# A graph layer on one core: weights prepared before the first rank on ScalarE, w1l and the first three x + beta on GpSimd

## The reference

```python
h = relu(layernorm(x))
agg = segment_sum(edge_attr, src, num_segments=50000)
g = silu(concat([h, agg], -1) @ W1 + b1)
g = g @ W2 + b2
g = (g - mean(g)) * rsqrt(var(g) + 1e-5) * gamma + beta
out = x + g + h
```

## Time and profile before

| | |
|---|---|
| median of three runs | 710.79 us |
| the profiled execution's own time | 710.52 us |
| its span, first to last instruction | 709.0 us |
| mean granted TensorE clock | 0.984 |
| busy: PE, PEld | 678.2 us (96%), 596.3 us (84%) |
| busy: DVE, ACT, POOL | 685.8 us (97%), 608.4 us (86%), 479.1 us (68%) |

### The profile page before, as it was taken

One profiled execution on the slowest core, in us unless ns is written; L12 is line 12 of the kernel. 1 busy time (PEld: TensorE's weight loads), 2 busy tenths in 40 slices (PEclk: granted clock), 3 DMA queues, 4 the chain that ended last, 5 costly groups with the idle time before them and its releaser, 6 DMA issues.

```text
span 709.0 us, 15612 instructions
## 1 busy us (share of the span) xinstructions
PE 678.2 (96%) x4566; PEld 596.3 (84%) x4566; DVE 685.8 (97%) x2361; ACT 608.4 (86%) x2090; POOL 479.1 (68%) x415
## 2 busy tenths in 40 slices
PE   5999988699999999999999999999999999999993
PEld 2888847599898989898989898999898989889993
DVE  6999879999999999999999999999999999999998
ACT  6999957589898989898989898989898988989883
POOL 5000057687778777777878777778777878777850
PEclk9999989999999999999999999999999999999997
DMA  6000001133333323242424242424232323331212
GB/s 221 1 2 2 1 15 54 52 116 108 112 113 107 118 97 130 87 137 84 140 83 142 83 139 85 141 83 140 85 135 87 129 96 120 106 106 52 81 43 84
DMA packets 28260, 65.90 MB, mean 93 GB/s; under 512 B 8469, under 2 KB 10023, under 8 KB 28174
## 3 DMA queue, kind: packets, MB, share of 16 engines
q1 hardware_dynamic: 15598, 51.90, 20.7%
q0 software_dynamic: 12576, 12.99, 7.5%
HBM read 52.05 MB, written 25.60 MB: 110 GB/s over the span
## 4 chain that ended last, share of the span: by engine, by line
DVE 66%; issue 20%; PE 10%; POOL 1%; DMA 1%; ACT 0%; DVEq 0%; POOLq 0%
DVE T L1138 14%; DVE lo L1126 10%; DVE stat L869 10%; DVE R L1108 8%; DVE R L1133 8%; PE y L671 3%; DVE R L1155 2%; PE za L658 2%; PE pre L665 2%; PE pre L658 2%; PE za L665 1%; DVE guess_off L922 1%; DVE mdd L905 1%; DVE var L908 1%; DVE guess L912 1%
## 5 line engine op out<-in xcount | busy, mean ns | idle before, releaser
L452 POOL DMA_INDIRECT G<-in_edge_attr_dram,slot_edge x388 | 465.2, 1199 | 120.9 <-issue 90.2
L754 PEld LDWEIGHTS y<-w2c,S 128*128 128x128 f32 (+1 forms) x1556 | 188.2, 191 | 8.0
L754 PE MATMUL y<-w2c,S 128*128 128x128 f32 (+1 forms) x1556 | 189.2, 275 | 0.0
L554 ACT ACTIVATE H<-X,shift,rstd 128x128 f32<-128x128 f32 x392 | 161.8, 489 | 4.1 <-DVE shift L927 4.1
L729 PE MATMUL pre<-hi,w1h 128*128 128x512 f32 (+1 forms) x392 | 163.7, 418 | 0.0
L730 PE MATMUL pre<-hi,w1l 128*128 128x512 f32 (+1 forms) x392 | 154.5, 394 | 0.0
L571 ACT ACTIVATE S<-pre,b1c 128x512 f32<-128x512 f32 (+1 forms) x196 | 125.3, 700 | 4.5 <-PE pre L734 4.5
L734 PE MATMUL pre<-lo,w1h 128*128 128x512 f32 (+1 forms) x392 | 122.7, 394 | 0.1
L1126 DVE TENSOR_TENSOR lo<-za,hi 128x1024 fp32r<-128x1024 f32 (+1 forms) x98 | 119.0, 1214 | 2.0 <-ACT hi L564 2.0
L869 DVE BATCH_NORM_STATS2 stat<-X 128x6 f32<-128x128 f32 x392 | 106.7, 280 | 0.1
L715 PE MATMUL za<-HOT,G 128*128 128x128 f32 (+1 forms) x784 | 104.8, 277 | 0.9 <-DMA G<-in_edge_attr_dram,slot_edge 0.9
(11 more groups left out here) (160 smaller groups left out, 947.5 us busy)
## 6 DMA issues: line engine op xcount, KB each, us to landing
X<-in_x_dram SPq DMA_DIRECT2D x48, 512.0 KB, 3.6
out_dram<-R SPq DMA_DIRECT2D x48, 512.0 KB
G<-in_edge_attr_dram,slot_edge POOLq DMA_INDIRECT x388, 2.5
X<-in_x_dram SPq DMA_DIRECT2D x1, 424.0 KB
out_dram<-R SPq DMA_DIRECT2D x2, 192.0 KB
w1f<-in_L_gnn_W_dram SPq DMA_DIRECT2D x1, 256.0 KB, 2.6
w2f<-in_L_gnn_W_dram SPq DMA_DIRECT2D x1, 128.0 KB, 2.5
srci<-in_src_dram SPq DMA_DIRECT2D x1, 87.5 KB
```

Of the source, the lines that this page charges most:

```text
L452: nc.gpsimd.indirect_dma_start(G[b.j][:, t, :], None, source, bass.IndirectOffsetOnAxis(ap=slot_edge[:, bass.ds(b.number(TILES, t), 1)], a ...
L554: done = nc.scalar.activation(H0[b.j][:, t, :], X[b.xj][:, t, :], ACT.Relu, bias=shift[b.j][:, t:t + 1], scale=rstd[b.ring(POWERS_LAG)][:, ...
L754: done = nc.tensor.matmul(places[t][0:r], S[c][:, m, t * r:(t + 1) * r], w2c[:, m, :], start=False, stop=True, skip_group_check=True)
```

## The change

ScalarE's preparation of the weights stands ahead of the first rank. GpSimd makes `w1l`, waiting for `w1h`, and `x + beta` for blocks 0, 1 and 2, each waiting for its block of `x`, between its trial DMA and its wait for that DMA. VectorE makes neither any more, and does `x + beta` from block 3 on.

```diff
@@ GpSimd
                 bounds_check=edge_limit, oob_is_err=False).then_inc(tried, 16)
+            pool.wait_ge(w1h_ready, 1)
+            nc.gpsimd.tensor_tensor(out=w1l[:], in0=w1f[:], in1=w1h[:].bitcast(F32),
+                                    op=ALU.subtract).then_inc(w1l_ready, 1)
+            for n in range(RING):
+                pool.wait_ge(x_loaded[n], 16)
+                nc.gpsimd.tensor_tensor(out=R[n][:], in0=X[n][:], in1=betas[:].unsqueeze(1).to_broadcast([P, TILES, D]),
+                                        op=ALU.add).then_inc(xb_done, 1)
             pool.wait_ge(tried, 16)
@@ ScalarE: the weights' block moves, its lines unchanged
             done.then_inc(gather_zeroed, 1)
+            act.wait_ge(weights_loaded, 16 * 6)
+            nc.scalar.copy(w1h[:], w1f[:]).then_inc(w1h_ready, 1)
+            for m in range(2):
+                nc.scalar.activation(junk_w[:, m, :], w2f[:, m, :], ACT.Copy, scale=-1.0 / D, accum_out=w2mean[:, m:m + 1])
...
+            nc.scalar.activation(b2c[:], b2f[:], ACT.Identity, bias=b2mean[:]).then_inc(w2c_ready, 1)
             def rank_of(column):
...
@@ VectorE, start of the block stage
             one_hots(Block(0))
-            dve.wait_ge(w1h_ready, 1)
-            nc.vector.tensor_tensor(out=w1l[:], in0=w1f[:], in1=w1h[:].bitcast(F32),
-                                    op=ALU.subtract).then_inc(w1l_ready, 1)
             split_low(Block(0), 0)
@@ VectorE, a block's step
-                x_plus_beta(b)
+                if b.n >= RING:
+                    x_plus_beta(b)
```

More of the change, by code:

```diff
@@ L513, in _ @@
             done.then_inc(gather_zeroed, 1)
+            act.wait_ge(weights_loaded, 16 * 6)
+            nc.scalar.copy(w1h[:], w1f[:]).then_inc(w1h_ready, 1)
+            for m in range(2):
+                nc.scalar.activation(junk_w[:, m, :], w2f[:, m, :], ACT.Copy, scale=-1.0 / D, accum_out=w2mean[:, m:m + 1])
+            nc.scalar.activation(junk_w[:, 2, :], b2f[:], ACT.Copy, scale=-1.0 / D, accum_out=b2mean[:]).then_inc(means_ready, 1)
+            act.wait_ge(means_ready, 1)
+            for m in range(2):
+                nc.scalar.activation(w2c[:, m, :], w2f[:, m, :], ACT.Identity, bias=w2mean[:, m:m + 1])
+            nc.scalar.activation(b2c[:], b2f[:], ACT.Identity, bias=b2mean[:]).then_inc(w2c_ready, 1)
             def rank_of(column):
@@ L536, in _ @@
             excess_of(1)
[L538 to L546, removed]
             def normalise(b, c):
```

## The result

The changed kernel takes 717.27 us (median of 4 runs, 717.18 to 717.36), the kernel before 710.76 in the same comparison: a ratio of 1.0091, 95% interval 1.008 to 1.0103, 6.5 us slower. The forecast was 715.6 in 710.2 to 719.0, slower. The profiled execution has a span of 715.6 us (before 709.0).

A forecast was written before the change was run, and what follows sets the result against it. VectorE's queue was taken as critical up to 27 us and as setting the pace in the block stage. A 7.2 us delay less 2.25 gained gave +5.0 on the profiled 710.52: 715.6 us forecast, range 710.2 to 719.0.

The forecast's parts named there:

- blocks 1 and 2 are worth 2.25 us: Block stage: taking x + beta of these two blocks off VectorE gains 2.25 us, between 1.1 and 2.25.
- the second 1.12 us: Block stage, block 2: removing x + beta moves VectorE up 1.12 us more, a lead that should last; lower end 0.
- The late ranks: Table stage start: ScalarE's first rank at 13.1 us, not 9.40, delays VectorE's first rank copy; cost 1.9 us, paid once.
- What delays VectorE before 27 us: Table stage up to 27 us: VectorE's queue is the critical path, so its delay reaches TensorE at 27.19 one for one.
- GpSimd's adds hold VectorE up: Early table stage: VectorE instructions wait for whole GpSimd instructions; 7.2 us delay, late ranks included; chance 0.50.
- the walk: Table stage, step by step from 12.45 us: GpSimd's adds move VectorE's word fields from 13.02 to 20.2, 7.2 us.
- the rule that I had weighed: VectorE with two SBUF inputs contends with GpSimd reading SBUF, two-port modes with any; the loser blocks for the whole instruction.
- my fill row: Price of GpSimd's adds from its fill, 392 elements in 0.81 us: 2.12 us per x + beta, 1.06 for w1l.
- The faster rival: Table stage: weights land while ScalarE idles, late ranks cost nothing, VectorE isn't held up; 708.4 us, chance 0.10.
- No hold-up: Table stage: GpSimd's adds leave VectorE alone; +1.9 - 2.25 = -0.3 us, 710.4 us, chance 0.20.
- slow adds: Table stage: GpSimd's adds take 4.2 us each; +14.5 - 2.25 = +12.2 us, 722.9 us, chance 0.07.
- a partial hold-up: Table stage: adds as short as VectorE's own, or VectorE slipping instructions between; +4.0 - 2.25 = +1.8, 712.5 us, chance 0.13.

The follow-up runs named there:

- experiment 2: Kernel before, with only the three x + beta moved to GpSimd; w1l stays on VectorE, weights' preparation behind the table stage: 716.13 us, ratio 1.0074.
- experiment 5: Kernel before, with VectorE's x + beta of blocks 0 and 1 moved into the table stage's tail, block 2 behind the totals: 708.73 us, ratio 0.9969.
- experiment 7: Kernel before, with the three x + beta on GpSimd late in the table stage, each waiting for a rank: 712.60 us, ratio 1.0023.
- experiment 8: Changed kernel, with each x + beta on GpSimd first waiting for a hot_tile of VectorE (group 3, 5, 7): 716.80 us, ratio 1.0083.
- experiment 1: Kernel before, with only ScalarE's weight preparation moved ahead of the first rank; w1l and all x + beta on VectorE: 712.69 us, ratio 1.0025.
- experiment 6: Changed kernel, with the three x + beta back on VectorE; w1l stays on GpSimd, weights prepared early: 713.06 us, ratio 1.0031.
- Experiment 4: Kernel before, with VectorE's own x + beta of blocks 0, 1 and 2 each moved one place earlier into VectorE's holes: 709.41 us, ratio 0.9979.

## Why the prediction was right, and where its size was off

- **`w1l` and block 0's add are worth nothing on VectorE, blocks 1 and 2 are worth 2.25 us.** Right within 0.5 us. The ramp gained 2.39 us in the changed kernel, and by the same row experiments 2, 5, 7 and 8 gained 2.06, 1.99, 1.80 and 2.16. TensorE didn't take the second 1.12 us back. Of `w1l` the trace shows it directly: the first `lo` now has 1.89 us of idle time ahead of it and not 1.28.

```profile
111.47 1.23 DVE L1133 TENSOR_TENSOR lo<-za,hi 128x1024 fp32r<-128x1024 f32 x1 [1.89 <-ACT hi L571]
```

- **The late ranks cost 1.9 us, once.** Right: 1.8 us of time in experiment 1, 2.15 at the end of the ranks.
- **They run at the same time as GpSimd's work and are hidden by it.** Right, and more than I had said. `w1l` on GpSimd and the late ranks together cost 1.91 us at the end of the ranks (experiment 6), less than the late ranks alone (2.15); the adds alone cost 7.05. The whole change costs 8.78, no more than 1.91 and 7.05 together. In the changed kernel group 0's last rank was there at 14.10 us, and the copy of it stood at 21.20 without a wait.
- **What delays VectorE before 27 us arrives whole at the end of the table stage.** Right: 8.77 us at 21.8, 8.78 at 97.5.
- **GpSimd's adds hold VectorE up.** Right in kind, 7.2 us in the prediction, 8.8 measured. This is the term of the sum that was mis-sized, and the walk that gave it was wrong in three steps. The word fields stood at 21.79 and not at 20.2, 1.59 us later. First, 0.44 us: an add takes 2.31 us (6.93 for three) and `w1l` 1.27, 8.2 us in all and not 7.4, and though they run without the gaps that I had put between them, VectorE goes on only at 20.64. Second, 0.56 us: I had `w1l` cost nothing, since VectorE would run until it stood for ranks anyway. But the hold begins before 11.95, and the sort step and the fields ahead of the rank copy came only behind it, from 20.64 to 21.20. Third, 0.59 us: I had let VectorE get through one or two instructions between two adds. It got through none, and what lies between the rank copy and the word fields came last, from 21.20 to 21.79. The profile that I had forecast has several holds of 1 to 2 us and the rank copy at 15.6; the trace has one of 9.05 and the copy at 21.20.

Of the rule that I had weighed from the Trainium skill's page "SBUF — State Buffer", section "Who interferes with whom", the half on two SBUF inputs against a GpSimd instruction that reads is now shown: `hot_tile` for 9.05 us, `hot_slot` for 2.48 us. The part on the whole instruction is too narrow for this case. VectorE stood for four GpSimd instructions in a row, and got in between none of them. The estimate from the Trainium skill's page "GPSIMD Engine Reference", section "3.1 Elementwise — side-by-side cycle accounting" (2.25 us an add) was nearer to the measured 2.31 than my fill row.

The faster rival needed the weights within 8.8 us; they came at 10.5. No hold-up, slow adds and a partial hold-up are excluded by the trace: VectorE stood for all of GpSimd's work, and an add took 2.31 us, neither 1.21 nor 4.2.

Left open: why the hold starts before the GpSimd instruction's record. It was seen in three kernels (the changed one, experiments 6 and 8); nothing here tells a hold that starts early from a record that starts late, since the profile's times on GpSimd are rough.

## What to carry to other kernels

An idle engine is not a free engine: here two-input adds moved to GpSimd, beside a VectorE that sets the pace with casts, tensor_scalars and two-input instructions, cost VectorE nearly GpSimd's whole time, 2.3 us for an add that VectorE does in 1.14. Look first for the moments at which the busy engine itself waits; here they held the same three adds at no cost and made the kernel 2.1 us faster. And a preparation that is moved ahead of a queue starts when its last input lands, not when the engine is idle.

## What the runs showed of the hardware that was not expected

- VectorE was locked out over several GpSimd instructions in a row: 9.05 us in one `hot_tile`, 7.16 us in one tensor_scalar of 0.16 us.
- The same the other way round: GpSimd's indirect DMA issues (1.00 us) wait for a VectorE instruction with two inputs in SBUF that started before them, and for the next one too if it follows at once. In the block stage before the change an issue with more than 0.2 us of them left took about 0.87 us more than what was left: 1.99 us at 113.62, beside the add of block 0 at 113.53, and 2.17 us here, where 1.31 us were left of two instructions in a row.

```profile
299.63 0.68 DVE L1155 TENSOR_TENSOR R<-T,R 128x512 f32<-128x512 f32 x1
300.24 1.22 DVE L1108 TENSOR_TENSOR R<-X,betas 128x1024 f32<-128x1024 f32 x1
301.37 1.22 DVE L1126 TENSOR_TENSOR lo<-za,hi 128x1024 fp32r<-128x1024 f32 x1
```

```profile
300.15 2.17 POOL L452 DMA_INDIRECT G<-in_edge_attr_dram,slot_edge  x1 [0.30 <-issue]
```

  Beside `lo`, whose one input `za` is in PSUM, the issues kept their 1.00 us. Experiment 4's longer issue is of this kind: 0.57 us were left of the add, and 0.57 + 0.86 = 1.43.
- The hold begins ahead of the GpSimd instruction's record: `hot_tile` due to end at 11.95 ended at 13.84, with `w1l` recorded from 12.39.
- Under fills VectorE's next five instructions still started at their usual distances and all ended at 15.4; under adds nothing started behind the held one.
- A GpSimd fill's time doesn't go by its number of elements: 0.99 us for 1024 in rows of 128, 0.81 us for 392 in rows of 8 (both float32), 0.81 us for 128 in pairs (float16). That the length of the rows decides was not tested by itself.
